# Probability-times-value products of two key blocks in one burst, and the first stage's buffers and five expert weights placed in the expert weights' memory

## The chip, the cores and the metric

The kernel runs on one core of a Trainium2 chip. The metric is the device time of one execution in microseconds (us), as the median of three runs: 2410.63 us before the change (2409.11 to 2410.94).

The engines are named as the profile names them: PE is TensorE (PEld are its weight loads), DVE is VectorE, ACT is ScalarE, POOL is GpSimd, and SP issues most DMAs. PSUM has eight banks of 128 x 512 fp32, which PE writes and DVE and ACT read.

## The reference

x has shape (2, 2048, 256). All of it is fp32.

```python
xn = layernorm(x)
q, k, v = heads(xn @ Wq.T + bq), heads(xn @ Wk.T + bk), heads(xn @ Wv.T + bv)   # 16 heads of 16
idx = clip(key - query, -128, 128) + 128
scores = (q k^T + q . rel_k[idx]) / 4
w = softmax(scores)
s = (w v + sum_k w * rel_v[idx]) @ Wo.T + bo
e = argmax(xn @ Wg + bg)                     # 8 experts, top 1
g = silu(gelu(xn @ W1[e]) @ W2[e])
out = x + s * g
```

## The kernel before, in words

The kernel has three stages, each a block of its own at whose end all engines meet: `project`, `attend` and `experts`.

**project** normalises x, computes q, k and v for 32 tiles of 128 tokens, splits q and k into three bf16 terms each, and writes them to DRAM. v is gathered in `v_all` and written by two DMAs of 2 MB on POOL's queue (line 231). At the end of the stage POOL waits until both have landed (line 232).

**attend** handles 32 pairs of head and batch ("blocks" n below), each with 16 query tiles and 16 key blocks of 128. It is one long software pipeline: every engine runs the same `loop(step)`, and the step at offset `off` does the parts of different ages. In the code `a` is the query tile whose scores are made for the row maxima, `x` (10 ahead) the tile whose relative scores are made, `t` (18 behind) the key block whose transposed scores and exponentials are made, `w` (19 behind) the key block whose values are summed, and `ended` (20 behind) closes a block. Within a step the work is done for four column parts u = 0 to 3 of 512 columns each. In each step:

- PE makes the scores of `a` for each u (line 976) into two PSUM banks `ps1`, and the transposed scores of `t` (line 990) into two banks `pst`; at u = 0 also the relative scores of `x` (line 998); at u = 1 the values of `w` (`key_values`, lines 940 to 955, recorded at line 924; at u = 2 where `w` is the first key block of a block n); at u = 2 the band's transposes (line 937); at the end of the step two window transposes (line 1013). The last step of a block n adds `near_values`, sixteen instructions, after u = 3. `weighted` (line 924) addresses the array in four tiles of 32 columns, one for each query quarter, so a value product stands beside three others.
- DVE reduces each part of the scores of `a` to a maximum (lines 1146 and 1148: the reduction over a part outside the band, and over the band, where the relative scores are added too), and signals `s1_used`. The scores of part u wait until the part two before has been used, since there are two `ps1` banks.
- ACT takes the exponentials of the four parts of `t` (line 1198) into `probs_T`, two buffers of one key block each; it copies the relative scores (line 1190), the transposed band (line 1182) and, every second step, two windows (line 1175), and at the end of the step takes the exponential of a band row (line 1211).
- POOL prepares bands, sides and shifts; SP moves bands and windows through DRAM.

DVE starts the stage with eight memsets of the rows of `k_left` and `k_right` that hold shifts (lines 1021 to 1026), then the routing of tokens to experts (from line 1037), then the loop.

**experts** projects the attention output (32 tiles), while SP loads eight w1 and eight w2 weights of 1 MB each (lines 1291 and 1293), and then runs 39 tiles of 128 tokens through their experts. The order of all work is written out by hand; there is no planner.

Of the kernel before, what the change touches and what calls it, by code (L numbers as in the profile page):

```python
# [5 lines left out]
F32 = mybir.dt.float32  # L6
# [6 lines left out]
P = 128  # L13
# [3 lines left out]
NB = S // P  # L17
# [67 lines left out]
def project(nc, io, dram, con, lg_all):  # L85
# [12 lines left out]
    with ExitStack() as ctx:  # L98
# [6 lines left out]
        x_all = sb("x_all", [P, TILES, D], F32)  # L105
# [11 lines left out]
        xn = [sb(f"xn{h}", [P, CT, D], F32) for h in range(2)]  # L117
        xT = [sb(f"xT{h}", [P, DC, CTOK], F32) for h in range(2)]
        qf = [[sb(f"qf{h}{u}", [P, CTOK], F32) for u in range(4)] for h in range(2)]
        terms = [[sb(f"terms{h}{u}", [P, 3, CTOK], BF16) for u in range(4)] for h in range(2)]  # L120
        v_all = sb("v_all", [P, HEADS, TILES, HD], F32)
# [15 lines left out]
        ident_set = sem("ident_set")  # L137
        stats_done = sem("stats_done")
# [15 lines left out]
        v_out = sem("v_out")  # L154
# [14 lines left out]
        with nc.Block() as block:  # L169
# [46 lines left out]
            def _(pool):  # L216
# [6 lines left out]

                v_pairs = dram["v"].rearrange("(h b) p i d -> b p h (i d)", b=B)
# [7 lines left out]
                pool.wait_ge(v_out, 16 * B)  # L232
# [200 lines left out]
def attend(nc, io, dram, con, lg_all, pos_i, expert_i, slots_filled, wo, bo, attn):  # L433
# [14 lines left out]
    with ExitStack() as ctx:  # L448
# [12 lines left out]
        k_left = two("k_left", [ALLROWS, S], BF16)  # L461
        k_right = two("k_right", [ALLROWS, S], BF16)
        rel = two("rel", [P, CH, WIN], F32)
        band = two("band", [P, NB, BAND], F32)
        pwin = two("pwin", [P, CH, NEARW], F32)
        pwin_T = sb("pwin_T", [P, 2, S], F32)
# [4 lines left out]
        probs_T = two("probs_T", [P, S], F32)  # L471
# [81 lines left out]
        shift_set = sem("shift_set")  # L553
# [97 lines left out]

        def score_bank(a, u):

            return pst[u % 2] if a.valid else (*pst, *ps1)[u]
# [3 lines left out]
        with nc.Block() as block:  # L658

            @block.sync  # L660
            def _(sp):
                def step(hb, off):
# [22 lines left out]
                    if off % NB == 4:  # L685
                        x = Step(hb, off)
                        if x.valid:
                            wait(sp, all_pv, x.count(1, -1))
                            wait(sp, v_built, x.count(1, 0))
                            sp.dma_start(v_raw, v_tab[x.n]).then_inc(v_in, 16)  # L690
# [36 lines left out]
                    if x.valid:  # L727
                        sp.wait_ge(sides_done, x.count(4, r + 1))
                        wait(sp, rel_in[x.par][r], x.count2(32 if r in (0, 3) else 16, 0))
                        sp.dma_start(dram["rel"][x.par, 4 * r:4 * r + 4].rearrange("s p w -> p s w"), rel[r % 2][:, :, :]).then_inc(rel_out[r], 16)  # L730

# [183 lines left out]
            def _(pe):  # L915
                def step(hb, off):
# [23 lines left out]
                    def key_values():  # L940
# [7 lines left out]
                        for nth in range(2):  # L948
                            for g in range(CH):
                                ps = all_pieces(w.s, g)  # L950
                                if nth < len(ps):
                                    kind, c0, c1 = ps[nth]
                                    mm = weighted(g, c0, c1, values[kind][:, w.s, :], probs_T[w.s % 2][:, g * CW + c0:g * CW + c1],
# [9 lines left out]
                    if t.valid and t.s == 0:  # L963
                        if at_start(hb) and t.n == 0:
                            pe.wait_ge(shift_set, 8)
                            pe.wait_ge(const_set, CONSTS + 3)
                        pe.wait_ge(back_in[t.par], t.count2(144, 144))
                        pe.wait_ge(rows_copied, t.count(4, 3))
                    for u in range(CH):
                        if a.valid:  # L970

                            if a.s == 0 and u == 0:
                                pe.wait_ge(qf_in[a.par], a.count2(48, 48))
                                pe.wait_ge(kf_in[a.par], a.count2(48, 48))
                            wait(pe, s1_used, a.count(64, 4 * a.s + u - 1))
                            nc.tensor.matmul(ps1[u % 2][:, :], q_front[a.par][:, a.s * P:(a.s + 1) * P], k_front[a.par][:, u * CW:(u + 1) * CW],  # L976
                                             start=True, stop=True).then_inc(s1_mm, 1)
# [40 lines left out]
            def _(dve):  # L1018

                for p in range(2):  # L1020
                    nc.vector.memset(k_left[p][ROWS:ALLROWS, :], 0.0).then_inc(shift_set, 1)
                    nc.vector.memset(k_right[p][ROWS:ALLROWS, :], 1.0).then_inc(shift_set, 1)
                dve.wait_ge(shift_set, 4)
                for p in range(2):
                    nc.vector.memset(k_left[p][ROWS:ROWS + 3, :], 1.0).then_inc(shift_set, 1)
                    nc.vector.memset(k_right[p][ROWS:ROWS + 3, :], 0.0).then_inc(shift_set, 1)
# [64 lines left out]
                def step(hb, off):  # L1091
# [26 lines left out]
                    def normalise():  # L1118
                        dve.wait_ge(den_ready, ended.count(1, 1))
                        nc.vector.tensor_tensor(attn[:, ended.n, :, :], turned[:, :, 0:HD], rv.unsqueeze(2).to_broadcast([P, NB, HD]),  # L1120
                                                ALU.mult).then_inc(norm_done, 1)

                    finish = (turn_out, denominators, normalise)
# [6 lines left out]
                    for u in range(CH):  # L1130
# [23 lines left out]
                        if ended.s == NB - 1 and ended.valid and u < 3:  # L1154
                            finish[u]()
# [4 lines left out]
            def _(act):  # L1160
                def step(hb, off):
# [16 lines left out]
                    def near_keys():  # L1178
# [3 lines left out]
                        nc.scalar.activation(probs_T[t.s % 2][:, c0:c1], pband[:, c0 - b0:c1 - b0], ACT.Copy).then_inc(bandT_evac, 1)  # L1182
# [9 lines left out]
                    if t.valid:  # L1192
                        wait(act, pv_done, t.count(16, t.s - 1))
                    for u in range(CH):
                        if t.valid:
                            act.wait_ge(st_mm, t.count(64, 4 * t.s + u + 1))
                            for _, c0, c1 in far_pieces(t.s, u):
                                ins = nc.scalar.activation(probs_T[t.s % 2][:, u * CW + c0:u * CW + c1], score_bank(a, u)[:, c0:c1], ACT.Exp, scale=SCALE)  # L1198
                            ins.then_inc(exp_done, 1)
                        if u == 0 and w.valid and w.s % 2 == 1:  # L1200
                            two_windows()
                        if u == 1 and x.valid:
                            relative()
                        if u == 2 and t.valid:
                            near_keys()
                    if y.valid:
# [6 lines left out]

                loop(step)


def experts(nc, io, dram, con, attn, expert_i, slots_filled, slots, wo, bo, out):

    SG, SR = 2, 4
    with ExitStack() as ctx:  # L1220
# [12 lines left out]
        w1 = sb("w1", [P, NE, DC, FF], F32)  # L1233
# [23 lines left out]
        w1_in = sem("w1_in")  # L1257
# [239 lines left out]
def build(nc, io, out):  # L1497
# [13 lines left out]
    with ExitStack() as ctx:  # L1511
# [5 lines left out]
        expert_i = sb("expert_i", [P, XT], I32)  # L1517
        attn = sb("attn", [P, NBH, NB, HD], F32)
# [4 lines left out]
        with ExitStack() as early:  # L1523
            lg_all = early.enter_context(nc.sbuf_tensor("lg_all", [P, TILES, NE], F32))
            project(nc, io, dram, con, lg_all)
            attend(nc, io, dram, con, lg_all, pos_i, expert_i, slots_filled, wo, bo, attn)
# [30 lines left out]
```

## Time and profile before

| | |
|---|---|
| Median of three runs | 2410.63 us (2409.11 to 2410.94) |
| The profiled execution's own time | 2410.91 us |
| Its span, first to last instruction | 2409.2 us |
| PE busy / PEld busy | 2303.6 us (96%) / 1159.1 us (48%) |
| DVE busy | 1694.8 us (70%) |
| ACT busy | 1767.1 us (73%) |
| POOL busy | 1356.6 us (56%) |
| Mean granted TensorE clock | 0.976 of full speed |

The execution's own time is 1.7 us over its span. A busy PE here is the union of its instructions from start to modelled end; matmuls are pipelined, so the next one starts before the one before has ended, and what PE can issue is read from the distance between starts. Roughly, `project` ends at 131 us, `attend` at 2036 us, and the rest is `experts`.

### The profile page before, as it was taken

What the parts mean: (1) busy time and instruction counts of PE and PEld (TensorE: products, weight loads), DVE (VectorE), ACT (ScalarE), POOL (GpSimd) and SP (SyncE); (2) the same over time, 40 slices, a digit from 0 to 9 for tenths busy, and PEclk for the clock granted to TensorE, in tenths of its full rate; (3) what the DMA queues carried; (4) which work ended last, traced back from release to release, by engine and by line L of the source; (5) the groups of instructions that cost most, each with busy time, mean ns of one, the idle gap of its engine ahead of it and who ended that gap; (6) DMA issues with size and microseconds to landing.
All of it is one profiled execution on the core that took longest, in us unless ns stands there. A gap on an engine that the chain in (4) does not pass through costs nothing. (4 is left out here: it accounts for less than half of the span.)

```text
span 2409.2 us, 46760 instructions
## 1 busy us (share of the span) xinstructions
PE 2303.6 (96%) x14320; PEld 1159.1 (48%) x14320; DVE 1694.8 (70%) x4408; ACT 1767.1 (73%) x4108; POOL 1356.6 (56%) x3283
## 2 busy tenths in 40 slices
PE   7839999999999999999999999999999998899998
PEld 4403444444444444444444444444444444667676
DVE  7678777777777777777777777777777761333333
ACT  5515888888888888888888888888888886221211
POOL 2326666666666666666666666666666666433332
PEclk9957999999999999999999999999999999999999
DMA  6667898788888888878888788878888762922221
GB/s 198 197 196 248 278 294 272 246 258 254 262 257 252 259 254 263 259 247 257 256 259 253 248 258 254 261 244 254 257 258 258 238 202 101 315 64 69 64 68 49
DMA packets 349605, 541.04 MB, mean 225 GB/s; under 512 B 29088, under 2 KB 257808, under 8 KB 349360
## 3 DMA queue, kind: packets, MB, share of 16 engines
q1 hardware_dynamic: 331904, 502.72, 66.4%
q0 software_dynamic: 17456, 35.33, 4.9%
q8 instruction: 120, 1.97, 0.3%
q14 instruction: 125, 1.02, 0.1%
HBM read 272.60 MB, written 269.43 MB: 225 GB/s over the span
## 5 line engine op out<-in xcount | busy, mean ns | idle before, releaser
L1148 DVE TENSOR_REDUCE part<-ps 128x1 f32<-128x512 f32 (+3 forms) x2048 | 1166.2, 589 | 371.8 <-PE ps L976 353.6
L1198 ACT ACTIVATE probs_T<-pst 128x256 f32<-128x256 f32 (+2 forms) x2012 | 1033.3, 528 | 175.2 <-PE pst L990 170.6
L976 PE MATMUL ps<-k_front,q_front 96*128 96x512 bf16 x2048 | 803.3, 392 | 25.8 <-DVE part L1146 20.4
L924 PE MATMUL pout<-probs_T,v_far 128*32 128x512 f32 (+3 forms) x4864 | 546.0, 535 | 7.7 <-ACT probs_T L1198 5.5
L976 PEld LDWEIGHTS ps<-k_front,q_front 96*128 96x128 bf16 x2048 | 197.2, 96 | 441.2 <-DVE part L1148 239.0
L990 PE MATMUL pst<-q_back,k_right 102*128 102x512 bf16 (+1 forms) x1012 | 344.3, 342 | 0.2 <-ACT probs_T L1198 0.2
L990 PE MATMUL pst<-q_back,k_left 102*128 102x256 bf16 (+1 forms) x1000 | 342.6, 343 | 0.0
L814 POOL TENSOR_TENSOR left<-left 128x256 f32<-128x256 f32 (+5 forms) x768 | 280.5, 365 | 60.2
L1211 ACT ACTIVATE band<-band,negm 128x384 f32<-128x384 f32 (+1 forms) x512 | 309.7, 605 | 0.0
L1146 DVE CUSTOM_DVE_ANT_0 band<-ps,band 128x256 f32<-128x256 f32 (+2 forms) x704 | 299.4, 425 | 0.0
L924 PEld LDWEIGHTS pout<-probs_T,v_far 128*32 128x32 f32 x4864 | 163.6, 108 | 248.8 <-issue 196.8
L1190 ACT ACTIVATE rel<-prel 128x257 f32<-128x257 f32 x512 | 209.7, 410 | 79.0 <-PE prel L998 79.0
L1182 ACT ACTIVATE probs_T<-pband 128x384 f32<-128x384 f32 (+1 forms) x512 | 242.5, 474 | 34.3 <-PE pband L937 31.9
L937 PE MATMUL pband<-ident,band 128*128 128x128 f32 x1472 | 247.1, 274 | 0.0
L880 POOL TENSOR_TENSOR rel<-rel,zero 128x1016 f32<-128x1016 f32 x128 | 240.9, 1882 | 0.0
L937 PEld LDWEIGHTS pband<-ident,band 128*128 128x128 f32 x1472 | 185.0, 141 | 100.2 <-issue 21.8
L1013 PE MATMUL psmall<-ident,pwin 128*128 128x128 f32 x1024 | 198.0, 274 | 0.0
L1013 PEld LDWEIGHTS psmall<-ident,pwin 128*128 128x128 f32 x1024 | 135.6, 142 | 108.0 <-issue 26.5
L840 POOL COPY q_back<-shT 6x128 bf16<-6x128 bf16 x512 | 146.7, 287 | 48.1 <-DVE shT L1128 6.9
L810 POOL TENSOR_TENSOR left<-band,left_mask 128x512 f32<-128x512 f32 x128 | 163.7, 1279 | 10.4 <-POOL q_back L840 0.4
L998 PE MATMUL prel<-rel_k,q_front 96*128 96x257 bf16 x512 | 143.9, 281 | 25.8 <-DMA q_front<-q_terms 21.9
L792 POOL TENSOR_TENSOR rel_ends<-rel,zero 128x8 f32<-128x8 f32 x128 | 26.2, 205 | 242.4 <-ACT rel L1190 242.2
(168 smaller groups left out, 2426.4 us busy)
## 6 DMA issues: line engine op xcount, KB each, us to landing
rel_scores<-rel SPq DMA_DIRECT2D x128, 1024.0 KB, 8.5
band_probs<-band SPq DMA_DIRECT2D x128, 768.0 KB, 4.0
pwin<-band_probs SPq DMA_DIRECT2D x128, 512.0 KB, 6.3
band<-rel_scores SPq DMA_DIRECT2D x64, 768.0 KB, 6.7
band<-rel_scores SPq DMA_DIRECT2D x64, 576.0 KB, 5.4
w<-in_w_dram SPq DMA_DIRECT2D x16, 1024.0 KB, 15.8
band<-rel_scores SPq DMA_DIRECT2D x64, 128.0 KB, 5.8
q_terms<-terms SPq DMA_DIRECT2D x48, 128.0 KB
```

The lines of the kernel that those rows point to most:

```text
L814: nc.gpsimd.tensor_tensor(left[:, :, 0:n], left[:, :, 0:n], left[:, :, n:2 * n], ALU.add).then_inc(left_link, 1)
L880: nc.gpsimd.tensor_tensor(sides, ends.unsqueeze(3).to_broadcast([P, CH, 2, M - 1]), zero_sides, ALU.add).then_inc(sides_done, 1)
L924: return nc.tensor.matmul(pout[32 * g:32 * g + 32, c0:c1], values, probs, start=first, stop=False, skip_group_check=True)
L937: mm = nc.tensor.transpose(pband[:, (i - t.s + 1) * P:(i - t.s + 2) * P], band[t.par][:, i, b * P:(b + 1) * P], con["ident"][:, :])
L976: nc.tensor.matmul(ps1[u % 2][:, :], q_front[a.par][:, a.s * P:(a.s + 1) * P], k_front[a.par][:, u * CW:(u + 1) * CW], start=True, stop=Tr ...
L990: mm = nc.tensor.matmul(score_bank(a, u)[:, c0:c1], k[:, t.s * P:(t.s + 1) * P], q_back[t.par][:, u * CW + c0:u * CW + c1], start=True, st ...
L1013: mm = nc.tensor.transpose(pnear[t.s % 2][:, b * P:(b + 1) * P], pwin[t.r % 2][:, t.g, b * P:(b + 1) * P], con["ident"][:, :])
L1146: ins = nc.vector.tensor_tensor_reduce(dst, src, dst, 1.0, LOWEST, ALU.add, ALU.max, peak)
L1148: ins = nc.vector.tensor_reduce(peak, src, AX_X, ALU.max)
L1182: nc.scalar.activation(probs_T[t.s % 2][:, c0:c1], pband[:, c0 - b0:c1 - b0], ACT.Copy).then_inc(bandT_evac, 1)
L1198: ins = nc.scalar.activation(probs_T[t.s % 2][:, u * CW + c0:u * CW + c1], score_bank(a, u)[:, c0:c1], ACT.Exp, scale=SCALE)
L1211: nc.scalar.activation(band[y.par][:, y.s, c0:c1], band[y.par][:, y.s, c0:c1], ACT.Exp, bias=negm[y.par][:, y.s:y.s + 1], scale=SCALE).the ...
```

## The change

**Values of two key blocks at a time.** `key_values` takes its key block as an argument. It is called only in steps where `w.s` is odd, at u = 1, twice: for the key block before and for `w`. `probs_T` gets a third buffer, picked by `key_block`, and ACT's wait on `pv_done` becomes one for the key block three back. **The third part's scores ahead.** In those steps the scores of `a` for u = 2 are issued before the two `key_values`, after the transposed scores of u = 1. **The band's exponential beside them.** In those steps ACT takes the band exponential (`band_exp`) after the relative scores at u = 1, in the others at the end as before. **`near_values`** moves from the end of the last step of a block to u = 1 of the next one, which has no values; `turn_out` and `denominators` on DVE move to u = 2 and 3, `normalise` to the end of the step.

**The other part.** `w1` is allocated for the whole kernel. `project` takes `x_all`, `xn`, `xT` and `qf` from its memory, and `v_all` is `attn`'s memory; `attend` takes `band[0]`, `rel`, `pwin` and `pwin_T` from `w1`. POOL no longer waits for `v_out` at the end of `project`; SP waits for it before the first load of v, and DVE before the first write of `attn`. The eight memsets of `k_left` and `k_right` move from DVE's start of `attend` to POOL's start of `project`. In the last block, at offset 36, SP loads w1 of experts 0 to 2 (after `band[0]`'s last use) and 3 to 4 (after `rel`'s); `experts` loads only 5 to 7, and then w2.

```diff
@@ tensor engine, in attend
-                    for u in range(CH):
-                        if a.valid:
-                            ...
-                            wait(pe, s1_used, a.count(64, 4 * a.s + u - 1))
-                            nc.tensor.matmul(ps1[u % 2][:, :], ...).then_inc(s1_mm, 1)
+                    def scores(u):
+                        ...
+                        wait(pe, s1_used, a.count(64, 4 * a.s + u - 1))
+                        nc.tensor.matmul(ps1[u % 2][:, :], ...).then_inc(s1_mm, 1)
+
+                    two_blocks = w.valid and w.s % 2 == 1
+                    for u in range(CH):
+                        if a.valid and not (two_blocks and u == 2):
+                            scores(u)
...
-                        if u == (2 if w.s == 0 else 1) and w.valid:
-                            key_values()
+                        if u == 1 and two_blocks:
+                            if a.valid:
+                                scores(2)
+                            key_values(Step(hb, off - LAG_T - 2))
+                            key_values(w)
                         if u == 2 and t.valid:
                             turn_band()
-                        if u == CH - 1 and w.s == NB - 1 and w.valid:
-                            pe.wait_ge(winT_evac, w.count(8, 8))
+                        if u == 1 and ended.s == NB - 1 and ended.valid:
+                            pe.wait_ge(winT_evac, ended.count(8, 8))
                             near_values(0)
                             near_values(1).then_inc(all_pv, 1)
@@ scalar engine
-                        wait(act, pv_done, t.count(16, t.s - 1))
+                        wait(act, pv_done, t.count(16, t.s - 2))
...
+                        if u == 1 and y.valid and two_blocks:
+                            band_exp()
...
+                    if y.valid and not two_blocks:
+                        band_exp()
@@ buffers of attend
-        probs_T = two("probs_T", [P, S], F32)
+        probs_T = [sb(f"probs_T{i}", [P, S], F32) for i in range(3)]
+        def key_block(x):
+            return probs_T[(x.n * NB + x.s) % 3]
@@ sync engine in attend
+                    if at_end(hb) and off == 2 * NB + 4:
+                        sp.wait_ge(bandT_mm, 16 * (NBH - 1))
+                        sp.wait_ge(left_ready, 4 * (NBH - 1))
+                        for r in range(4):
+                            sp.wait_ge(prob_out[r], 16 * (NBH - 1))
+                        load_experts(0, EARLY)
+                        for r in range(4):
+                            sp.wait_ge(rel_out[r], 16 * NBH)
+                        load_experts(EARLY, LATER)
@@ gpsimd in project
+                for p in range(2):
+                    pool.memset(con["k_left"][p][ROWS:ALLROWS, :], 0.0).then_inc(shift_set, 1)
+                    pool.memset(con["k_right"][p][ROWS:ALLROWS, :], 1.0).then_inc(shift_set, 1)
...
-                pool.wait_ge(v_out, 16 * B)
@@ sync engine in experts
-                for e in range(NE):
+                for e in range(NB * BAND // (DC * FF) + 2, NE):
                     sp.dma_start(w1[:, e], ...).then_inc(w1_in, 16)
```

## Rows read from the trace of the kernel before

**Rows 1.** Busy time of each engine in one block n (sixteen steps); stretch, length, busy.

```profile
1019.72:1077.00 57.28, 56.94 (x390) 26.61 (x391) 45.29 (x120) 50.67 (x121) 35.98 (x94) 1.00 0.80 252
```

**Rows 2.** Timeline of PE, one step: start us, us, engine, line, operation.

```profile
1043.11 1.07 PE L924 MATMUL pout<-probs_T,v_far 128*32 128x512 f32 x8
1044.11 0.39 PE L976 MATMUL ps<-k_front,q_front 96*128 96x512 bf16 x1
...
1044.45 0.49 PE L937 MATMUL pband<-ident,band 128*128 128x128 f32 x3
1044.77 0.38 PE L976 MATMUL ps<-k_front,q_front 96*128 96x512 bf16 x1
...
1045.21 0.38 PE L1013 MATMUL psmall<-ident,pwin 128*128 128x128 f32 x2
1045.43 0.38 PE L976 MATMUL ps<-k_front,q_front 96*128 96x512 bf16 x1
...
1045.98 0.38 PE L976 MATMUL ps<-k_front,q_front 96*128 96x512 bf16 x1
1046.20 0.38 PE L990 MATMUL pst<-q_back,k_right 102*128 102x512 bf16 x1
1046.51 1.07 PE L924 MATMUL pout<-probs_T,v_far 128*32 128x512 f32 x10
```

**Rows 3.** Timeline of PE: first and last value bursts of the block, and near_values.

```profile
1019.72 1.06 PE L924 MATMUL pout<-probs_T,v_far 128*32 128x128 f32 x10
...
1067.40 1.07 PE L924 MATMUL pout<-probs_T,v_far 128*32 128x512 f32 x10
...
1072.97 1.92 PE L924 MATMUL pout<-pwin_T,rv_win 128*32 128x512 f32 x16
1074.82 0.44 PE L1013 MATMUL psmall<-ident,pwin 128*128 128x128 f32 x2
...
1076.33 0.39 PE L976 MATMUL ps<-k_front,q_front 96*128 96x512 bf16 x1 [0.25 <-DVE part L1146]
...
1077.01 1.07 PE L924 MATMUL pout<-probs_T,v_far 128*32 128x128 f32 x10
```

**Rows 4.** Timeline of DVE; idle before an instruction and its releaser in brackets.

```profile
1042.45 0.30 DVE L1128 STREAM_TRANSPOSE shT<-shb 128x128 bf16<-128x128 bf16 x1
...
1044.53 0.29 DVE L1148 TENSOR_REDUCE part<-ps 128x1 f32<-128x128 f32 x1 [0.60 <-PE ps L976]
...
1045.21 1.93 DVE L1148 TENSOR_REDUCE part<-ps 128x1 f32<-128x512 f32 x3
1047.93 0.43 DVE L1148 TENSOR_REDUCE part<-ps 128x1 f32<-128x256 f32 x1 [0.79 <-PE ps L976]
...
1076.19 0.08 DVE L1146 DVE_READ_ACCUMULATOR2_ANT part<- 128x1 f32 x1
```

**Rows 5.** Timeline at the start of attend: POOL, DVE and SP (SPq).

```profile
117.94 1.20 POOL L231 DMA_DIRECT2D v_pairs<-v_all  x1
132.05 0.91 DVE L1021 MEMSET k_left<- 6x1024 uint32 x1 [15.70 <-PEq L169]
144.89 0.18 DVE L1037 CAST pwin_T<-iota_i 128x39 f32<-128x39 int32 x1
146.11 0.49 SPq L715 DMA_DIRECT2D band<-rel_scores  x1
...
160.45 0.42 DVE L1148 TENSOR_REDUCE part<-ps 128x1 f32<-128x256 f32 x1
```

**Rows 6.** DMA issues: count, KB each, median us from issue to landing.

```profile
k_terms<-terms POOLq DMA_DIRECT2D x48, 128.0 KB, 4.8
...
band<-rel_scores SPq DMA_DIRECT2D x64, 128.0 KB, 5.8
```

**Rows 7.** Waits of 2030 to 2110 us: engine, line, releaser: us in total, times, longest.

```profile
DVE s_rows L1454 <- DMA x_and_s<-s_rows: 15.8, 8, 7.2
PE py L1390 <- DMA w<-in_w_dram: 0.8, 1, 0.8
```

More of the change, by code:

```diff
@@ L82, in chain, with project @@
     return link
-def project(nc, io, dram, con, lg_all):
+def project(nc, io, dram, con, lg_all, w1, attn, v_out):
     CT = 4
@@ L430, in _, with attend @@
                 values(CHUNKS - 1, 1)
-def attend(nc, io, dram, con, lg_all, pos_i, expert_i, slots_filled, wo, bo, attn):
+def attend(nc, io, dram, con, lg_all, pos_i, expert_i, slots_filled, w1, w1_in, wo, bo, attn, v_out):
     with ExitStack() as ctx:
@@ L460, in attend @@
         q_back = two("q_back", [ALLROWS, S], BF16)
[L461 to L466, printed above, removed]
+        k_left, k_right = con["k_left"], con["k_right"]
+        EARLY = NB * BAND // (DC * FF)
+        LATER = EARLY + 2
+        band = [w1[:, 0:EARLY].rearrange("p e c f -> p (e c f)").rearrange("p (i w) -> p i w", w=BAND), sb("band1", [P, NB, BAND], F32)]
+        rel = [w1[:, EARLY + i].rearrange("p c f -> p (c f)").rearrange("p (i w) -> p i w", w=WIN) for i in range(2)]
+        pwin = [w1[:, LATER, i].rearrange("p (r w) -> p r w", w=NEARW) for i in range(2)]
+        pwin_T = w1[:, LATER + 1:NE].rearrange("p e c f -> p e (c f)")
         left = sb("left", [P, CH, P], F32)
@@ L730, in step, with load_experts @@
                         sp.dma_start(dram["rel"][x.par, 4 * r:4 * r + 4].rearrange("s p w -> p s w"), rel[r % 2][:, :, :]).then_inc(rel_out[r], 16)
+                def load_experts(first, last):
+                    for e in range(first, last):
+                        sp.dma_start(w1[:, e], io["w1"][e].rearrange("(c p) f -> p c f", p=P)).then_inc(w1_in, 16)
                 q_tab, k_tab, v_tab = dram["q_terms"], dram["k_terms"], dram["v"]
@@ L1018, in _ @@
             def _(dve):
[L1020 to L1026, printed above, removed]
                 v = nc.vector
@@ L1190, in relative, with band_exp @@
                         nc.scalar.activation(rel[x.r % 2][:, x.g, M:M + RELS], prel[:, 0:RELS], ACT.Copy).then_inc(r_evac, 1)
-                    if t.valid:
-                        wait(act, pv_done, t.count(16, t.s - 1))
-                    for u in range(CH):
[L1195 to L1206, printed above, removed]
+                    def band_exp():
                         bl = band_blocks(y.s)
@@ L1517, in build @@
         expert_i = sb("expert_i", [P, XT], I32)
+        w1 = sb("w1", [P, NE, DC, FF], F32)
+        w1_in = ctx.enter_context(nc.semaphore("w1_in"))
+        v_out = ctx.enter_context(nc.semaphore("v_out"))
         attn = sb("attn", [P, NBH, NB, HD], F32)
@@ L1524, in build @@
             lg_all = early.enter_context(nc.sbuf_tensor("lg_all", [P, TILES, NE], F32))
-            project(nc, io, dram, con, lg_all)
-            attend(nc, io, dram, con, lg_all, pos_i, expert_i, slots_filled, wo, bo, attn)
-        experts(nc, io, dram, con, attn, expert_i, slots_filled, slots, wo, bo, out)
+            for name in ("k_left", "k_right"):
+                con[name] = [early.enter_context(nc.sbuf_tensor(f"{name}{i}", [ALLROWS, S], BF16)) for i in range(2)]
+            project(nc, io, dram, con, lg_all, w1, attn, v_out)
+            attend(nc, io, dram, con, lg_all, pos_i, expert_i, slots_filled, w1, w1_in, wo, bo, attn, v_out)
+        experts(nc, io, dram, con, attn, expert_i, slots_filled, slots, w1, w1_in, wo, bo, out)
 _INS = ["x", "wqT", "wkT", "wvT", "wg", "bq", "bk", "bv", "bg", "rel_kT", "rel_v", "woT", "bo", "w1", "w2"]
```

73 lines of the change are left out of this document (51 added, 22 removed).

## The prediction

> **What bounds the kernel now.** I read the page's busy shares, then one block n (16 steps, 57.3 us, 32 of them) as a window, then the timelines of PE, DVE and ACT in it, and last the two ends of attend. In the block PE is busy 56.94 of 57.28 us, ACT 50.67, DVE 45.29 [rows 1]. The reader should see in PE's timeline that the starts lie back to back: scores and the transposed scores behind them take 0.44 together (1044.77 to 1045.21), so 0.22 each, band transposes 0.32, window transposes 0.22, first to second scores of a step 0.55, and a value burst 1.00 with 0.31 instead of 0.22 between the last bf16 matmul and it; the whole step is 3.40 us and has no hole [rows 2]. Seven pairs of steps take 1067.40 - 1019.72 = 47.68, 6.81 a pair; the two steps that hold near_values take the other 9.61 [rows 3]. So PE's issue sets the pace, but only just: DVE waits once in each step, for the scores behind the burst, 0.60 and 0.79 [rows 4], and about 12 us in the block (57.28 - 45.29) [rows 1]. It is a loop: scores land, DVE reduces, and with two ps1 banks the scores two further on may go.
>
> The Trainium skill, "Perfetto Trace Analysis", section "Identifying the Most-Contended Engine", says that matmul busy time doesn't tell TensorE's headroom and LDWEIGHTS busy does. Here that is 26.61 of 57.28 us, which would leave PE half free, and then taking time from PE would give nothing. The starts in [rows 2] say otherwise for the kernel before; I go by them.
>
> **What the burst costs, and what pairing takes away.** near_values has 16 instructions and takes 1.85 to the next start (1072.97 to 1074.82) [rows 3], where 8 or 10 take 1.00 [rows 2]. Two key blocks in one burst are such a row: 1.85 instead of 2.00, and one entry of 0.09 less. That is 0.24 a pair of steps, if PE stays the bound. That is eight bursts less in a block n, over 30.9 blocks in the steady part (offsets 18 to 511 are 494 steps, 247 pairs): 59 us.
>
> **What is late next.** The burst is now 1.85 without new scores instead of 1.00 twice, and the step without a burst gives PE only some 2.3 us of work (3.40 - 1.00 - 0.09), while DVE has about 2.6 in any step: three plain parts take 1.93 [rows 4], which I read as 0.62 from start to start and 0.69 for the last; a part that the band splits takes 0.68 (1044.53 to 1045.21) [rows 4]. So in the step without a burst DVE is the bound, PE can't run ahead by more than two banks, and in the other PE is. I follow one pair, at zero the scores of u = 3 behind a double burst:
> - They reach DVE 0.42 later (1044.11 to 1044.53) [rows 2, 4]. Then DVE has six parts without a rest: u = 3, the four of the next step, and u = 0 of the one after. PE has all of them ready in time: scores of the next step's u = 0 at 0.66 and u = 1 at 1.21 (transposed 0.22, windows 0.22, and 0.55 [rows 2]).
> - Three plain and two split parts from start to start, 3 x 0.62 + 2 x 0.68 = 3.22, then 0.69: DVE ends u = 0 at 0.42 + 3.22 + 0.69 = 4.33. PE starts on that 0.06 later (1076.27 to 1076.33) [rows 3, 4]: 4.39. This is the third part's scores, put ahead of the burst, and they can't go earlier.
> - The shift transpose, 0.30 in every second pair [rows 4], lies in the chain, as the step after offset 4k has no burst: 0.10 to 0.15 a pair. The row maximum falls into the gap. I take 4.50.
> - Entry 0.31, burst 1.85, transposed scores 0.22, band transposes 0.32 [rows 2, 3], and only then the scores of u = 3: 2.70.
>
> The pair is 7.20 us against 6.81: +0.39. Said as DVE's rest: it now waits twice for about 0.7; afterwards once, from about 1.2 after the scores of u = 2 (two parts) to 2.70 + 0.42, so 1.9. The scores ahead save it from a worse case, but u = 3 stands behind the burst and the band's transposes. Over 247 pairs +96 us. Bounds: 7.0 (no shift transpose in the chain, transposed scores of 128 columns behind the burst) is +47; 7.5 (ACT late as well, below) is +170.
>
> near_values moves into the step without a burst, at u = 1: there DVE does two parts under it, and turn_out and the reciprocal behind it. Its pair is now 9.61 - 6.81 = 2.80 longer than the others [rows 3]; I leave that, since the longer burst gap and the work of DVE behind it add about what the removed entry gives; bounds -0.5 to +1 a block, -15 to +30 us, kept in the range.
>
> **ACT.** It has 50.67 us of work in 57.28, 6.33 a pair [rows 1]. In 7.20 it has 0.9 to rest. At a double burst it has u = 1's exponentials, the relative copy and now the band's; that covers most of 1.85. The third probs_T buffer means that it never waits for the values. So I count nothing for it, up to +0.3 a pair in the upper bound. The two extra waits of key_values (exponentials and band of both blocks) are met: the transposed scores of u = 1 already wait for the last exponential of the step before.
>
> **The ends.** Start of attend: DVE starts at 132.05, 15.70 after its last work, when the 2 MB of v issued at 117.94 have landed [rows 5]. k's DMAs, issued before, land 4.8 after issue [rows 6], at about 122.7; v's share their queues. Without the wait I take 5 us earlier (3 to 9). DVE's memsets take from 132.05 to 144.89, 12.8 us, and then routing to 160.45, the first part [rows 5]. They go to POOL at a time when it waits for the first k. But the first part also needs the band's load, issued at 146.11 [rows 5] and landing 5.8 later [rows 6], at 151.9, and that doesn't depend on the memsets: 160.45 - 151.9 = 8.5 at most. Together 13.5 at most; I take 12 (5 to 17), as a few early steps then meet other loads. The waits for v_out that SP and DVE get stand hundreds of us behind the landing.
>
> Early weights: 5 of 16 MB leave the start of experts. There DVE waits 15.8 us for the landing of s_rows and PE 0.8 for w2 [rows 7]; most of the first is the start of the transfer, where the 11 MB left still stand, and PE works off a part of it. I take 3 (0 to 9). In the last block these 5 MB lie ahead of the last bands and windows on SP's queue: I count nothing, up to +5 if the windows come late. The last 16 steps have no scores of `a`, so there the saving of 0.24 holds: 2 us.
>
> **Sum.** The profiled execution took 2410.91, its span 2409.2, the median of the runs is 2410.63, 0.3 lower. 2410.9 + 96 - 12 - 3 - 2 = 2490. Own bounds: 2411 + 47 - 24 = 2434 to 2411 + 170 - 8 = 2573.
>
> **Rivals.**
> - PE stays the bound: then -0.24 x 247 = -59, less the ends' 17: 2335. For it: PE is busy 99% [rows 1], back to back [rows 2]. Against it: it needs DVE to do six parts in 6.81 - 0.24 - 2.70 - 0.48 = 3.4 us, 0.57 a part, where no part takes less than 0.62. With the present small waits of PE gone too (some 0.1 a pair) it would be 2310. Chance 0.14.
> - The two effects cancel in the loop (pairs of 6.7 to 6.9), as some parts have less work than I gave, and only the ends are left: 2411 - 17 = 2394. It needs 0.4 less in the chain. Chance 0.08.
> - ACT becomes the bound too, on the slower side: behind a double burst its exponentials of u = 2 can't start before the burst's end plus about 0.6, and its work up to there is 6.33 plus one start-up a burst. It decides when that passes 7.20, and then costs about 0.3 a pair more: 2490 + 74 = 2564. For it: ACT is busy 88% of the block [rows 1], more than DVE. Chance 0.10.
> - Mine, 0.68.
>
> **Chances and range.** Faster by more than 0.2% (5 us, what a measurement of this kernel can tell): the first rival and most of the second, 0.20. Same: 0.03. Slower: 0.77. My own case alone spans 2440 to 2550. Downward the range takes in the second rival, 2390; what is left out is the first rival and the upper tail of the third.
>
> **What would show it.** Right: DVE's idle before the scores of line 976 comes once in two steps, 1.7 to 2.0 long; starts of double bursts 7.1 to 7.3 apart; PE waiting on DVE (line 1148) in the steps without a burst; a block of 60 us; first DVE part at about 148; the double burst 1.85 to the next start. Wrong: bursts 6.6 apart and DVE's wait split or short; then either the parts are quicker than 0.62 or PE doesn't need what I put between the burst and u = 3. If ACT's idle is gone and the bursts are over 7.4 apart, the third rival holds.

## The result: slower by 3.7%

The changed kernel takes 2498.99 us (median of 4 runs, 2496.57 to 2499.64), the kernel before 2410.26 (4 runs, 2409.11 to 2410.94): a ratio of 1.0366, 95% interval [1.0353, 1.0379]. The profiled execution's span is 2497.4 us against 2409.2, 88.2 more. I had said 2490.

near_values, once in each block n, cuts the span into pieces that can be compared (the first instruction of its 16, in each trace). Its place in the block is another after the change, so the pieces at either end hold a little of that shift too:

| Piece | before | after | difference |
|---|---|---|---|
| project, to SP's first load of attend | 131.78 | 136.48 | +4.70 |
| from there to the first score part | 28.67 | 22.22 | -6.45 |
| first part to the first near_values | 110.55 | 115.09 | +4.54 |
| 29 whole blocks, to the third last near_values | 1661.21 | 1749.35 | +88.14 |
| the last two near_values | 54.81 + 44.85 | 56.05 + 41.63 | -1.98 |
| last near_values to the first matmul of experts | 4.94 | 7.23 | +2.29 |
| from there to the end | 372.3 | 369.3 | -3.0 |

Attend has lost 93.0 us from its first score part on, nearly all of it at an even pace of 3.04 a block. Its start has brought 1.75 instead of 12, and experts 3.0, where I had put 3.

The window of one block after, near_values to near_values as in [rows 1] (stretch, length, then busy time of PE, PEld, DVE, ACT, POOL; granted clock; DMA share; GB/s):

```profile
997.47:1057.77 60.30, 57.39 (x392) 28.61 (x391) 43.98 (x120) 50.89 (x120) 35.83 (x95) 1.00 0.75 241
```

PE's rest was 0.34 us in a block before and is 2.9 now, and DVE rests 16.3 instead of 12. No engine is busy all the time. That is how a closed loop between two engines looks. PE's timeline over one pair shows it (compare [rows 2]):

```profile
1010.30 0.39 PE L1017 MATMUL ps<-k_front,q_front 96*128 96x512 bf16 x1 [0.28 <-DVE part L1192]
1010.62 1.92 PE L968 MATMUL pout<-probs_T,v_far 128*32 128x384 f32 x18
1012.48 0.39 PE L1036 MATMUL pst<-q_back,k_left 102*128 102x512 bf16 x1
1012.70 0.49 PE L981 MATMUL pband<-ident,band 128*128 128x128 f32 x3
1013.03 0.38 PE L1017 MATMUL ps<-k_front,q_front 96*128 96x512 bf16 x1
...
1014.86 0.39 PE L1017 MATMUL ps<-k_front,q_front 96*128 96x512 bf16 x1 [0.18 <-DVE part L1192]
...
1017.55 0.39 PE L1017 MATMUL ps<-k_front,q_front 96*128 96x512 bf16 x1 [0.28 <-DVE part L1192]
1017.87 1.92 PE L968 MATMUL pout<-probs_T,v_far 128*32 128x512 f32 x20
```

And DVE's over the same pair ([rows 4] before):

```profile
1010.84 0.69 DVE L1192 TENSOR_REDUCE part<-ps 128x1 f32<-128x512 f32 x1
1013.45 1.68 DVE L1192 TENSOR_REDUCE part<-ps 128x1 f32<-128x512 f32 x3 [1.93 <-PE ps L1017]
...
1016.06 1.90 DVE L1192 TENSOR_REDUCE part<-ps 128x1 f32<-128x512 f32 x3
```

Read it as a ring. The scores of u = 3 go at 1013.03, DVE takes them 0.42 later and works without a rest until it frees the bank for the next scores of u = 2, at 1017.55. That is 4.52. Those scores stand directly ahead of the double burst, so the burst waits for DVE too, and the next scores of u = 3 stand behind it: 0.32 + 1.86 + 0.22 + 0.33, 2.7. Together 7.25. In that second stretch DVE has work only until 1011.53, for u = 1 and then for the u = 2 that goes at 1010.30. It rests from there until the scores of u = 3 reach it at 1013.45, which is the 1.93.

The groups of the page after say the same over the whole run (line, engine, operation; busy, mean ns; idle before, and releaser):

```profile
L1192 DVE TENSOR_REDUCE part<-ps 128x1 f32<-128x512 f32 (+3 forms) x2048 | 1140.4, 586 | 502.3 <-PE ps L1017 496.1
L1017 PE MATMUL ps<-k_front,q_front 96*128 96x512 bf16 x2048 | 804.0, 393 | 103.0 <-DVE part L1192 49.9
L968 PE MATMUL pout<-probs_T,v_far 128*32 128x512 f32 (+3 forms) x4864 | 493.8, 530 | 0.5 <-ACT probs_T L1253 0.4
```

DVE waits 496.1 us for scores, where it waited 353.6 before. The bursts' own busy time, 493.8 us, did get shorter (546.0 before), and nothing of it arrived.

### The profile page after: what moved, and what is told of

Its sections match the earlier page's. It is cut to its first block and busy times, and to the rows that moved or that the text cites. A ratio compares the mean times of both kernels' runs of the same rounds, so it can differ in the third digit from the quotient of the medians.

```text
span 2497.4 us, 46765 instructions
## 1 busy us (share of the span) xinstructions
PE 2317.5 (93%) x14320; PEld 1221.0 (49%) x14320; DVE 1648.3 (66%) x4400; ACT 1773.0 (71%) x4108; POOL 1365.8 (55%) x3291
## 5 line engine op out<-in xcount | busy, mean ns | idle before, releaser
L1192 DVE TENSOR_REDUCE part<-ps 128x1 f32<-128x512 f32 (+3 forms) x2048 | 1140.4, 586 | 502.3 <-PE ps L1017 496.1
L968 PE MATMUL pout<-probs_T,v_far 128*32 128x512 f32 (+3 forms) x4864 | 493.8, 530 | 0.5 <-ACT probs_T L1253 0.4
L1236 ACT ACTIVATE w<-prel 128x257 f32<-128x257 f32 x512 | 209.8, 410 | 71.9 <-PE prel L1044 68.5
L924 POOL TENSOR_TENSOR w<-w,zero 128x1016 f32<-128x1016 f32 x128 | 240.8, 1881 | 0.0
L1062 PE MATMUL psmall<-ident,w 128*128 128x128 f32 x1024 | 196.3, 272 | 2.4 <-POOL w L844 2.4
L1062 PEld LDWEIGHTS psmall<-ident,w 128*128 128x128 f32 x1024 | 137.7, 141 | 89.9 <-POOL w L844 3.1
L1036 PEld LDWEIGHTS pst<-q_back,k_left 102*128 102x128 bf16 x1000 | 97.4, 97 | 135.6 <-issue 103.1
L1243 ACT ACTIVATE band<-band,negm 128x384 f32<-128x384 f32 (+1 forms) x256 | 163.2, 638 | 0.0
L1243 ACT ACTIVATE w<-w,negm 128x384 f32<-128x384 f32 (+1 forms) x256 | 162.8, 636 | 0.0
L1221 ACT ACTIVATE w<-psmall 128x512 f32<-128x512 f32 x256 | 160.3, 626 | 0.0
L1190 DVE CUSTOM_DVE_ANT_0 w<-ps,w 128x256 f32<-128x256 f32 (+2 forms) x352 | 149.3, 424 | 0.0
```

The costliest lines, as they stand in the source:

```text
L924: nc.gpsimd.tensor_tensor(sides, ends.unsqueeze(3).to_broadcast([P, CH, 2, M - 1]), zero_sides, ALU.add).then_inc(sides_done, 1)
L968: return nc.tensor.matmul(pout[32 * g:32 * g + 32, c0:c1], values, probs, start=first, stop=False, skip_group_check=True)
L1036: mm = nc.tensor.matmul(score_bank(a, u)[:, c0:c1], k[:, t.s * P:(t.s + 1) * P], q_back[t.par][:, u * CW + c0:u * CW + c1], start=True, st ...
L1062: mm = nc.tensor.transpose(pnear[t.s % 2][:, b * P:(b + 1) * P], pwin[t.r % 2][:, t.g, b * P:(b + 1) * P], con["ident"][:, :])
L1192: ins = nc.vector.tensor_reduce(peak, src, AX_X, ALU.max)
L1221: nc.scalar.activation(pwin_T[:, :, both].rearrange("p b (k c) -> p b k c", k=2), psmall[:, :].rearrange("p (k b c) -> p b k c", k=2, b=2) ...
```

## The experiments

All were timed against the kernel before, whose median in these jobs was 2409.8 to 2411.2.

| Kernel | us, median | ratio, 95% interval | block |
|---|---|---|---|
| after | 2498.99 | 1.0366 [1.0353, 1.0379] | 60.30 |
| ends_only | 2407.05 | 0.9987 [0.9977, 0.9996] | 57.28 |
| no_ahead | 2398.18 | 0.9943 [0.9926, 0.9959] | 56.98 |
| sc3_first | 2505.17 | 1.0388 [1.0370, 1.0405] | 60.40 |
| dve_half | 2389.57 | 0.9903 [0.9886, 0.9919] | 56.83 |
| act_end | 2537.51 | 1.0536 [1.0517, 1.0554] | 61.50 |
| ends_half | 2368.78 | 0.9835 [0.9819, 0.9852] | 56.25 |
| spread | 2396.39 | 0.9947 [0.9933, 0.9961] | 56.98 |
| v_late | 2396.17 | 0.9944 [0.9929, 0.9958] | 56.98 |
| tail | 2395.57 | 0.9945 [0.9930, 0.9960] | 56.99 |
| tail_v | 2400.51 | 0.9951 [0.9937, 0.9964] | 56.99 |

### ends_only: the other part of the change alone

```diff
-                        if u == 1 and two_blocks:
-                            if a.valid:
-                                scores(2)
-                            key_values(Step(hb, off - LAG_T - 2))
-                            key_values(w)
+                        if u == (2 if w.s == 0 else 1) and w.valid:
+                            key_values(w)
```

(and the third part's scores, near_values, turn_out, normalise, the band's exponential and ACT's wait on `pv_done` back where they were; the third `probs_T` buffer stays).

> The other half of the change alone: memory, memsets on POOL, no wait for v's landing, early w1 weights; the values one key block a step as in the kernel before. By the prediction's terms it gains 12 + 3 us: 2396. By the trace of the kernel after it gains next to nothing, since project runs 5 us longer there under the memsets and the windows come late in the last block: 2404 to 2412. A block n takes 57.28 us again in either case. If the block were above 57.5, part of the loss in the loop would come from the shared memory and not from the pairing.

Measured 2407.05, 3 to 4 us under before, and the block is 57.28 to the hundredth. So the whole loss is in the order of the loop, not in the shared memory, and the ends are worth about a quarter of what I gave them.

### no_ahead: the third part's scores back behind the burst

```diff
-                        if a.valid and not (two_blocks and u == 2):
+                        if a.valid:
                             scores(u)
...
                         if u == 1 and two_blocks:
-                            if a.valid:
-                                scores(2)
                             key_values(Step(hb, off - LAG_T - 2))
```

> The kernel after, with the third part's scores behind the double burst as in the other steps. My theory (a loop through DVE with two banks, and what PE issues between the burst and the next scores): DVE still gets two parts to do under the burst (u = 0 and 1 instead of 1 and 2), but the first scores behind the burst no longer stand behind the transposed scores and the band's transposes (0.22 + 0.32). Followed a pair takes 6.90 instead of 7.25: 2499 - 0.35 x 247 = 2412, range 2395 to 2425, DVE's longest idle about 1.5. The rival, that scores ahead feed DVE and so shorten its gap, as they are meant to: without them a pair is longer by about one part, 0.6, so 2640.

Measured 2398.18, in the range of 2395 to 2425 and far from the rival's 2640: 101 us less than after, from one matmul in every second step moved from ahead of the burst to behind it. This is the most telling run. PE's timeline of it, around a double burst:

```profile
1033.44 0.38 PE L1017 MATMUL ps<-k_front,q_front 96*128 96x512 bf16 x1
1033.81 1.92 PE L968 MATMUL pout<-probs_T,v_far 128*32 128x512 f32 x20
1035.67 0.39 PE L1017 MATMUL ps<-k_front,q_front 96*128 96x512 bf16 x1
...
1040.67 1.92 PE L968 MATMUL pout<-probs_T,v_far 128*32 128x512 f32 x18
```

and DVE's one wait of that pair:

```profile
1036.09 0.42 DVE L1190 TENSOR_REDUCE part<-ps 128x1 f32<-128x256 f32 x1 [1.21 <-PE ps L1017]
```

The scores ahead of the burst are now those of u = 1, which go without a wait for DVE, and so does the burst. Behind it scores follow at once, 2.23 after the last ones instead of 2.73. DVE rests 1.21 instead of 1.93, and the pair takes 6.86. My sentence that "the scores ahead save it from a worse case" is refuted: they made the case. Putting a matmul that needs a bank of DVE's in front of the long burst makes the burst itself wait for DVE.

### sc3_first: u = 3's scores as the first behind the burst

```diff
-                        if a.valid and not (two_blocks and u == 2):
+                        if a.valid and not (two_blocks and u >= 2):
                             scores(u)
+                        if a.valid and two_blocks and u == 2:
+                            scores(3)
```

> The kernel after, with the scores of u = 3 issued first behind the double burst, ahead of the transposed scores of u = 2 and the band's transposes. My theory: DVE's idle falls from 1.9 to about 1.35, but the scores of u = 0 of the next step now wait for all of PE's displaced work, so that DVE rests 0.5 there instead; by hand a pair is 7.1 instead of 7.25: 2470, range 2450 to 2490. If the distance from the burst to the next scores were the whole story: 2499 - 0.54 x 247 = 2366.

Measured 2505.17, no gain at all. DVE's waits in one pair, whose bursts start at 1079.93 and 1087.24 (7.31 apart):

```profile
1082.21 0.69 DVE L1194 TENSOR_REDUCE part<-ps 128x1 f32<-128x512 f32 x1 [1.38 <-PE ps L1017]
1083.42 1.02 DVE L1194 TENSOR_REDUCE part<-ps 128x1 f32<-128x512 f32 x2 [0.51 <-PE ps L1017]
```

The long wait is shorter by 0.55, the 0.22 and 0.33 that now stand behind. But 0.51 comes back one part later: the scores of the next step's u = 0 start 3.07 behind the burst's start, as they do in after, and DVE still has five parts from there to the bank that the next burst's scores wait for. PE's weight loads now wait for ACT as well, between 500 and 1900 us (releaser: us in total, times, longest; in after the same wait is 0.8 us, 3 times):

```profile
PEld pst L1038 <- ACT probs_T L1255: 92.1, 303, 0.6
```

So both expectations failed. The term "transposed scores 0.22, band transposes 0.32" is in the ring, yet taking it out doesn't shorten the ring, since a second path of the same length runs through the scores of u = 0; how much ACT's share adds wasn't measured alone. It also separates two readings of no_ahead: scores right behind the burst alone bring nothing, as long as other scores still stand ahead of it.

### dve_half: DVE's plain parts over half the columns

```diff
-  ins = nc.vector.tensor_reduce(peak, src, AX_X, ALU.max)
+  ins = nc.vector.tensor_reduce(peak, src[:, 0:len(sel) * P // 2], AX_X, ALU.max)
```

It leaves half of each row out of the maxima outside the band; all else is the kernel after.

> The kernel after, with each row maximum outside the band taken over the first half of its columns only, so a plain part takes about 0.34 instead of 0.60 on DVE (this leaves out part of the maxima; all other work is the same). My theory, the pair is set by six parts on DVE plus 2.7 of PE and the latencies: with short parts the chain is under PE's own 6.45 to 6.6, so 2499 - 0.7 x 247 = 2325, range 2300 to 2350, a block about 54.5 to 55. The rival that ACT holds the pair at 7.2: not faster than 2485. If PE's back-to-back issue of the kernel before (6.81) were a floor: 2395.

Measured 2389.57, 109 us less than after. DVE was the slow side of the ring, as I had it. But 2325 was far off, and what PE's weight loads wait for between 500 and 1900 us shows why (releaser: us in total, times, longest):

```profile
PEld pst L1036 <- ACT probs_T L1253: 197.9, 494, 0.8
```

The same row in after:

```profile
PEld pst L1036 <- ACT probs_T L1253: 0.8, 3, 0.4
```

Behind DVE, ACT stands at once. It isn't full either: its work is 50.6 us of the block.

### ends_half: the same cut on ends_only

```diff
@@ on ends_only
-  ins = nc.vector.tensor_reduce(peak, src, AX_X, ALU.max)
+  ins = nc.vector.tensor_reduce(peak, src[:, 0:len(sel) * P // 2], AX_X, ALU.max)
```

> The ends-only kernel (values one key block a step) with the row maxima outside the band over half their columns (leaves out part of the maxima). It asks how far DVE holds the single bursts, and what stood in the way of the half-column run of the pairs (block of 56.83, not 54.5). PE's own issue in a block of the kernel before is 57.28 less some 1.5 to 1.8 of small waits for DVE: block 55.5 to 55.8, time 2350 to 2365. If this is below the pairs' 56.83, double bursts cost more than they save even with DVE out of the way, and what is late then is ACT; if it stays at 57 or more, PE's waits for DVE were nothing and a block needs all of 57 us on PE.

Measured 2368.78, block 56.25 against 56.83 in dve_half. With DVE's parts short in both, single bursts beat double ones by 0.58 a block, as long as the double ones have scores ahead of them. The saving that the double burst has in PE's issue (1.85 instead of 2.00, [rows 3]) doesn't arrive in that order. The short parts weren't tried on no_ahead, so whether they would bring my rival "PE stays the bound", 2335, there isn't shown; with the scores ahead they don't.

### act_end: the band's exponential at the end of every step

```diff
-                        if u == 1 and y.valid and two_blocks:
-                            band_exp()
...
-                    if y.valid and not two_blocks:
+                    if y.valid:
```

> The kernel after, with the band's exponential at the end of every step, as before the change, and not beside the double burst. If DVE's loop alone sets the pair of 7.25, ACT has some 0.3 to 0.9 of slack in it and the time stays at 2499. If ACT is close behind, as the half-column run suggests (there PE waits on ACT before the transposed scores), 0.5 of ACT's work comes off the burst, where it was free, and onto the stretch after it: up to 0.2 to 0.4 a pair more, 2550 to 2600.

Measured 2537.51, between the two times expected, and block 61.50. "The band's exponential beside the burst" is worth 38.5 us in this kernel: without it ACT rests longer through the double burst (11.8 us in a block instead of 9.4) and is late behind it. The wait that was 0.8 us in after, in the same stretch of 500 to 1900:

```profile
PEld pst L1036 <- ACT probs_T L1253: 41.5, 115, 0.5
```

One exponential of 0.6 us, misplaced in each pair, costs the pair 1.20 / 8 = 0.15. So ACT's slack, which I gave as 0.9 a pair, isn't free everywhere in the pair.

### spread, v_late, tail, tail_v: the start, on the better order

All four are no_ahead with the early weights at offset 42 instead of 36. spread has POOL's memsets in twos between k's DMAs:

```diff
                         stacks_out(pool, 1, c0, 0)
+                        shift_sets(pair_i)
                         stacks_out(pool, 1, c0 + 1, 1)
```

> no_ahead (scores of u = 2 behind the double burst) with two repairs of the ends: POOL's eight memsets in twos between k's DMAs, away from DVE's normalisation, and the five early w1 loads at offset 42, after the last window load. In the trace after, DVE's normalisation of the first tiles took 5.48 under the memsets instead of 2.67, and PE waited 1.87 + 0.54 for windows in the last block. If these are the causes: project ends 4 to 5 us earlier, 2.4 less in the last block, 2398 - 6.5 = 2391 to 2393, provided that the start of the loop follows the end of project. If the weights at offset 42 no longer land before the stage ends, 1 to 2 of it is lost again. The rival for the first, that the later end of project comes from buffers in other memory: 2396.

v_late adds to it that the second DMA of v is issued at POOL's start of attend:

```diff
+                    if b == 0:
                         pool.dma_start(v_pairs[b], ...).then_inc(v_out, 16)
...
+                pool.dma_start(v_pairs[1], ...).then_inc(v_out, 16)
                 zero_sides = ...
```

> spread, with v's second DMA of 2 MB issued at POOL's start of attend instead of at the end of project. Without the wait for v the stage still ended 15 us after DVE's last work. If what it waits for is q's and k's terms, held up by v's traffic on the same DMA engines, the stage ends 5 to 8 us earlier; the first DVE part then comes 3 to 8 us earlier, 2384 to 2390. If it is the landings of their own packets, nothing: the same as spread, or 1 to 3 worse, as v's traffic then meets the first loads of attend.

tail has the memsets on DVE, behind its last work of project:

```diff
                 products(CHUNKS - 1, 1)
+                for p in range(2):
+                    v.memset(con["k_left"][p][ROWS:ALLROWS, :], 0.0).then_inc(shift_set, 1)
...
```

> The kernel of spread (scores of u = 2 behind the double burst, early weights at offset 42), but the eight memsets run on DVE, behind its last work of project, instead of on POOL in the middle of project. DVE has nothing for 12 to 15 us there, so they should cost nothing (about 12 us, from about 116.5 to 129). Theory (POOL's work slows DVE's in project, and the chain that the band's load ends is 22 us long from SP's first load of attend to the first score part): project's DVE work ends at 116.4 as in the kernel before, SP starts attend at about 131.5, the first part at about 154, and the time is 2392 to 2394, against 2396.4 for spread. Rival (the later start of attend is another effect of the double use of memory, for example waits on xn's or qf's buffers): DVE ends at 120 again, SP starts at 135, the time is that of spread.

tail_v is tail with v's second DMA behind that of the empty slots:

```diff
                         pool.dma_start(dram["slots"]..., empty[:, :, :]).then_inc(slots_set, 16)
+                        pool.dma_start(v_pairs[1], ...).then_inc(v_out, 16)
```

> tail, with v's second DMA (1 MB) issued on POOL behind the DMA of the empty slots, about 15 us into attend, instead of at the end of project. Theory: k's DMAs no longer share the queues with it, so attend starts 4 us earlier (127.5), and the relative scores and the band's load are issued before v takes the queues, so that their chain stays 22 us: first part at about 150, time 2388 to 2390, 4 us under tail. Rival (as when v was issued at attend's start: what is not waited for in project collides with the relative scores instead): first part no earlier than in tail, same time.

Measured 2396.39, 2396.17, 2395.57 and 2400.51. The first three can't be told apart. Their traces say more than their times:

| us | before | after | no_ahead | spread | v_late | tail | tail_v |
|---|---|---|---|---|---|---|---|
| normalising of the last pair of chunks starts (DVE) | 82.43 | 86.60 | 86.69 | 86.81 | 86.96 | 82.07 | 83.04 |
| ACT waits for q_terms' landing | 3.6 | 4.8 | 7.0 | 0 | 1.8 | 5.9 | 6.4 |
| SP's first load of attend | 131.78 | 136.48 | 139.94 | 135.16 | 131.03 | 135.60 | 140.39 |
| from there to the first part | 28.67 | 22.22 | 22.22 | 22.24 | 26.27 | 22.11 | 22.20 |

Three things follow.
- POOL's memsets cost project 4 us. In after, DVE at its first normalising and the small scalings ahead of it:

```profile
9.61 1.29 DVE L284 TENSOR_SCALAR mean<-mean 128x8 f32<-128x8 f32 x1
...
12.93 5.48 DVE L306 TENSOR_SCALAR w<-w,mean,rstd 128x256 f32<-128x256 f32 x8
```

The same in before:

```profile
9.43 0.17 DVE L262 TENSOR_SCALAR mean<-mean 128x8 f32<-128x8 f32 x1
...
11.48 2.67 DVE L284 TENSOR_SCALAR xn<-x_all,mean,rstd 128x256 f32<-128x256 f32 x8
```

and POOL in after at that time:

```profile
9.07 1.80 POOL L243 MEMSET k_left<- 3x2048 bf16 x1
10.82 1.85 POOL L244 MEMSET k_right<- 3x2048 bf16 x1
12.61 1.82 POOL L243 MEMSET k_left<- 3x2048 bf16 x1
14.38 1.95 POOL L244 MEMSET k_right<- 3x2048 bf16 x1
```

In spread the first normalising is 2.67 again, but the memsets hit later ones:

```profile
86.81 4.39 DVE L306 TENSOR_SCALAR w<-w,mean,rstd 128x256 f32<-128x256 f32 x4 [0.81 <-DMA x_norm<-w]
```

with this on POOL:

```profile
86.72 1.80 POOL L242 MEMSET k_left<- 3x2048 bf16 x1
88.46 1.95 POOL L243 MEMSET k_right<- 3x2048 bf16 x1
```

With no memset on POOL, in tail, DVE is where it was in before (82.07).
- tail still gained nothing over spread. It normalises 4.7 earlier, but then waits 5.9 where spread waits 0: ACT's bias of the seventh chunk waits for the landing of q_terms. That is 3.6 us in before and 5.9 and 6.4 in the two kernels without memsets on POOL. What makes that landing vary by some 3 us between kernels that issue the same DMAs is open. Against "they should cost nothing", DVE's memsets end only 2.9 us before attend starts in tail and 4.9 before in tail_v (at 135.45), so the later v couldn't show there; whether they stood on the path in either isn't shown.
- The 22.2 us are DVE's routing, not the band's load, as my expectation for tail had it. In after the first part follows it without a gap:

```profile
146.54 0.42 DVE L1090 COPY w<-pband 128x256 f32<-128x256 f32 x1 [6.91 <-PE pband L1006]
...
158.60 0.18 DVE L1128 CAST expert_i<-w 128x39 int32<-128x39 f32 x1
158.70 0.42 DVE L1192 TENSOR_REDUCE part<-ps 128x1 f32<-128x256 f32 x1
```

Only in v_late is it the band. There attend starts 4.1 us before spread's, but ACT then waits 8.67 for relative scores to land in DRAM, while v's transfer runs (that it is v which holds them up is argued), and the first part comes at the same time, behind a wait for the band.

```profile
157.30 0.43 DVE L1194 TENSOR_REDUCE part<-ps 128x1 f32<-128x256 f32 x1 [3.79 <-DMA w<-rel_scores]
```

## Why the prediction was right, and where it wasn't

- **The ring, right in mechanism and size.** The chain worked out was 4.50 + 2.70 = 7.20. The trace has 4.52 + 2.73, and the eight double bursts of the block 997 to 1058 (1003.32 to 1053.74) are 7.20 apart on average. The double burst takes 1.86 to the next start (1.85 said), DVE rests once in two steps, 1.93 long (1.7 to 2.0 said), and the block is 60.30 (60 said). Loop and last steps together brought +93.0 against +96 - 2 = 94. DVE's rests in that block are 1.5 to 2.0, a little wider than said.
- **near_values, right.** I left its pair 2.80 longer than the others. It is 60.30 - 50.42 - 7.20 = 2.68.
- **PE's load time against its starts.** The prediction set the Trainium skill ("Perfetto Trace Analysis", section "Identifying the Most-Contended Engine") against the back-to-back starts. Both had a share: the starts did lie 0.22 apart and set the pace before, but time taken from PE's bursts brought 0.30 a block at best (no_ahead, 56.98 against 57.28) of the 1.9 that eight times 0.24 would be. So that rule came nearer than the starts to what the saving was worth. But its reason, a PE that is half free, isn't what the runs show: PE's starts do lie back to back, and DVE and ACT stand right behind it.
- **ACT, right for this kernel, with less room than said.** No wait of PE for ACT is large in after. act_end and dve_half show that it is next.
- **"The scores ahead save it from a worse case", wrong.** The sum for the kernel as it stands was right, but the judgement on its parts wasn't: no_ahead is the better case, by 101 us. I had followed the ring with the scores ahead, and never the one without them.
- **Start of attend, -12 said, -1.75 measured; the failed term of the sum.** Two errors. "5 us earlier" without the wait for v was +4.70. DVE's last work of project ended at 116.35 before and at 121.70 after, and SP's first load of attend came 15.4 and 14.8 behind it: dropping the wait brought 0.7, and DVE's later end cost 5.3. v's transfer itself holds the end, not the wait for it: in v_late, where its second half isn't issued before the stage ends, attend starts 4.1 earlier than in spread. And "at a time when it waits for the first k" looked at POOL's idle time and not at what DVE does then. "8.5 at most" from the memsets was 6.45. They did hide something: PE did its relative matmuls beside them, before the routing's. Now the routing's matmul stands behind those on PE, and DVE waits 6.91 for it. So the first DVE part came at 158.70 and not "at about 148".
- **Early weights, -3 said, -3.0 in this profile, and not firm.** DVE's wait for s_rows fell from 15.8 [rows 7] to 7.1, and from the first matmul of experts on the kernel takes 369.3 instead of 372.3. That piece is 368.3 to 372.7 in all the changed kernels, ends_only's is 370.5, so one profile doesn't settle the size.
- **"Up to +5 if the windows come late": they did, but not by the early weights.** PE in the last block of after:

```profile
2102.03 0.44 PE L1062 MATMUL psmall<-ident,w 128*128 128x128 f32 x2 [1.87 <-POOL w L844]
2112.20 0.44 PE L1062 MATMUL psmall<-ident,w 128*128 128x128 f32 x2 [0.54 <-POOL w L844]
```

  ends_only issues the same weights at the same offset, and PE has no such wait there. Issued six steps later, in spread, the long wait is still 1.88. What PE waits for is POOL's last small copy into the windows, and POOL has the routing's indirect DMAs ahead of it, eight in four steps, one after another:

```profile
2099.55 0.96 POOL L953 DMA_INDIRECT slot_tokens<-tok_i,pos_i  x1 [0.30 <-issue]
2100.81 0.96 POOL L953 DMA_INDIRECT slot_tokens<-tok_i,pos_i  x1 [0.31 <-issue]
2101.77 0.20 POOL L844 COPY w<-left_sum 128x4 f32<-128x4 f32 x1
2111.95 0.20 POOL L844 COPY w<-left_sum 128x4 f32<-128x4 f32 x1
```

  The last two of these copies are 10.18 apart in after and 10.17 in ends_only. POOL keeps its pace, and with double bursts PE gets through four steps of the last block fast enough to meet it.

The nine us between 2490 and 2499 are thus the start of attend (10.25 too hopeful) less the loop and its last steps (1 too gloomy).

## What to carry to other kernels

When two engines hand buffers to each other, write the ring down, instruction by instruction, and do it for the neighbouring orders too: one matmul moved from behind a long burst to ahead of it turned a gain of 0.5% into a loss of 3.7%, since it made the burst wait for the other engine. Work that merely moves to an idle engine is not free, if another engine shares what it uses, and work that is removed may have covered a third engine's. A ring can be slower than each engine in it: here 60.3 us a block, with PE busy for 57.4 of them, ACT for 50.9 and DVE for 44.0. Speeding up one engine showed the next one at once.

The best version is no_ahead with the early weights later, at 2395.6 to 2396.4 (ratio 0.9945, [0.9930, 0.9960] for tail), a gain of half a per cent. Its 2 to 3 us under no_ahead are within the scatter of the runs.

## What the runs showed of the hardware

DVE's TENSOR_SCALAR from SBUF to SBUF stops while POOL does a memset: 0.17 us becomes 1.29, eight of 128x256 take 5.48 instead of 2.67, four take 4.39 instead of 1.4. The statistics on 128x256 (2.71 for eight), TENSOR_TENSOR and small reciprocals keep their times beside the same memsets. The Trainium skill, "SBUF — State Buffer", section "SBUF: two separate sides", says that DVE and GpSimd share one pair of ports as an exclusive lock, and that a DVE operation in a two-port mode blocks for the whole GpSimd instruction. The trace agrees: the 1.29 us scaling starts at 9.61, and it and the two behind it end at 10.90 to 10.92, just after POOL's memset, which runs from 9.07 to 10.87. What the first scaling loses, 1.12, a later one's 0.29 and the normalising's 2.81 make up the 4.2 us.

The other surprise is how much one step's placement on ACT is worth. The exponential that act_end moves is 0.56 to 0.69 us long in after, ACT is busy 50.9 of 60.3 us, and the move costs 1.2 us a block.
